# Layer norm 1 of a small vision transformer read from PSUM, with the position rows folded into the patch products, and a new order of work behind it

## What is computed

```python
h = einsum('bnf,of->bno', patches, W) + b + pos_emb           # 768 -> 256
h = h + attention(layernorm(h))      # 16 heads of 16, causal with ALiBi bias, inside each image
h = h + ffn(layernorm(h))
# ffn: r = relu(bitlinear(x, w_fc) + gate * (x @ v.T @ fast_b.T @ u.T)); bitlinear(r * r, w_proj)
# bitlinear(x, w): w rounded to -1, 0, 1 times a scale of its row; layernorm without gain, eps 1e-5
```

## Time and profile before

| | us |
|---|---|
| median of 3 runs | 68.41 (68.33 to 68.67) |
| the profiled execution, its own time | 68.16 |
| its span in the trace | 66.4 |
| TensorE busy | 58.6 |
| VectorE busy | 45.3 |
| ScalarE busy | 38.6 |
| GpSimd busy | 25.9 |

### The profile page before, as it was taken

The page is one execution under the profiler, slowest core; times in us unless marked ns, Lnnn a source line. Parts: engine busy times, 40 slices in busy tenths (PEclk is TensorE's granted clock), DMA queues, the critical chain, the costliest instruction groups (busy, mean ns, idle before and its releaser), DMA issues.

```text
span 66.4 us, 2165 instructions
## 1 busy us (share of the span) xinstructions
PE 58.6 (88%) x894; PEld 53.1 (80%) x894; DVE 45.3 (68%) x97; ACT 38.6 (58%) x78; POOL 25.9 (39%) x43
## 2 busy tenths in 40 slices
PE   5989999999989999999947958999988999999900
PEld 5968588889968999698936846999978999999800
DVE  0000039467999896999799993725999589989660
ACT  5300012824294969974899699830988599783000
POOL 6500007597779569999957100000000000000840
PEclk9999999999999999999999999999999999999996
DMA  0899999999810000000000000000000000000044
GB/s 0 238 352 340 320 392 400 344 387 400 320 42 0 10 0 0 0 10 0 10 0 0 10 5 5 0 10 0 0 0 0 0 0 0 0 0 0 10 161 156
DMA packets 3371, 6.50 MB, mean 98 GB/s; under 512 B 385, under 2 KB 1314, under 8 KB 3362
## 3 DMA queue, kind: packets, MB, share of 16 engines
q1 hardware_dynamic: 3218, 6.24, 26.4%
q10 hardware_dynamic: 144, 0.13, 0.6%
HBM read 5.85 MB, written 0.52 MB: 96 GB/s over the span
## 4 chain that ended last, share of the span: by engine, by line
PE 60%; DVE 18%; ACT 10%; DMA 5%; issue 3%
PE psum L307 12%; PE psum L467 12%; PE psum L493 11%; PE psum L373 5%; PE psum L347 5%; DMA head_sb<-head 5%; PE psum L313 3%; PE psum L402 3%; DVE z L787 3%; PE psum L476 2%; PE psum L327 2%; DVE prob_n L850 2%; DVE bn L779 2%; DVE prob_t L857 2%; ACT zt_hi L610 2%
## 5 line engine op out<-in xcount | busy, mean ns | idle before, releaser
L1051 POOL TENSOR_TENSOR tail_sb<-tail_sb,h 128x256 f32<-128x256 f32 x3 | 2.1, 734 | 25.0 <-DVE tail_sb L886 25.0
L493 PE MATMUL psum<-mlp_t,sq_lo 128*128 128x256 f32 x32 | 7.7, 281 | 0.0
L493 PE MATMUL psum<-mlp_t,sq_hi 128*128 128x256 f32 x32 | 7.7, 280 | 0.0
L601 ACT ACTIVATE std<-mv,eps_sb 128x1 f32<-128x1 f32 x8 | 2.4, 294 | 8.8 <-DVE mv L781 8.8
L777 DVE TENSOR_TENSOR h<-psum,posb 128x256 f32<-128x256 f32 x4 | 1.6, 412 | 8.5 <-PE psum L307 8.5
L467 PE MATMUL psum<-zt_hi,fc_t 128*128 128x256 f32 x32 | 6.9, 287 | 0.5 <-ACT zt_hi L610 0.5
L726 ACT ACTIVATE head_sb<-psum,fc_scale 128x256 f32<-128x256 f32 x16 | 6.7, 471 | 0.7 <-DVE kqv_sb L897 0.7
L467 PE MATMUL psum<-zt_lo,fc_t 128*128 128x256 f32 x32 | 6.7, 279 | 0.0
L493 PEld LDWEIGHTS psum<-mlp_t,sq_lo 128*128 128x128 f32 x32 | 6.0, 189 | 0.0
L493 PEld LDWEIGHTS psum<-mlp_t,sq_hi 128*128 128x128 f32 x32 | 6.0, 189 | 0.0
L307 PE MATMUL psum<-head_sb 128*128 128x256 f32 x24 | 5.7, 389 | 0.3 <-DMA head_sb<-head 0.3
...
## 6 DMA issues: line engine op xcount, KB each, us to landing
...
```

The costliest lines, as they stand in the source:

```text
L493: mm = pe.matmul(mlp_ps[f * BH + b], part[:, n % RING, a, b * P:(b + 1) * P], mlp_t[:, 2 * j + a, :], start=j == 0 and a == 0 and i == 0 a ...
L601: nc.scalar.activation(std[:, which, b:b + 1], mv[:, which, b, 1:2], ACT.Sqrt, bias=eps_sb[:, 0:1]).then_inc(std_ready, 1)
```

## The change

- The position rows are stored twice, 17 rows from partition 0 and again from partition 32 (49 rows in all). ACT rounds them to fp32r, DVE replaces the lower copy's vectors by the low part, and one fp32r product for each block adds both to `tok_ps[b]` as the last of its sum. The fp32 product L509 and `posb` are gone.
- `stats1` and `normalise1` read `tok_ps[b]` in PSUM. ACT copies each block to h (`hidden_copy`) behind its z; the products that reuse these banks wait for the copies, and so does `residual`.
- DVE spreads no keys: ACT takes heads 0 and 3 of half 0, POOL heads 1 to 3 of half 1. DVE copies k of half 1, which was ACT's. ACT makes `ident_bf` and `select_r`, which were POOL's.
- DVE's order: z of block 3 ahead of the key copy, both `fc_sums` ahead of the low part of the second turned z, `rows_sum(0)` behind the two divisions.
- Layer norm 2: both std ahead of `mlp_signs(0)`, the copy of the turned z ahead of `duo_rows(1)`, `mlp_signs(1)` later. On TensorE `turn_mlp(1)` stands behind `project(1)`, `hidden_low(0, 0)` ahead of it, `mlp_out(0, 0)` ahead of `hidden_main(1, 0)`.
- POOL squares step 0 (`SQ_POOL`), DVE the other seven; `residual(1)` moves behind POOL's weight work.

```diff
+POS_LOW = 32
+POS_ROWS = POS_LOW + S + 1
...
-        posb = sb("posb", [P, E])
+        pos_sb = sb("pos_sb", [POS_ROWS, P + E])
+        pos_r = sb("pos_r", [POS_ROWS, P + E], F32R)
...
-        z2t_ps = [bank[2], bank[3]]
-        low_ps = [bank[2][:, 0:HT], bank[4][:, 0:HT]]
-        FCB = [bank[i] for i in (0, 1, 2, 0, 5, 1, 2, 0)]
+        z2t_ps = [bank[1], bank[3]]
+        low_ps = [bank[1][:, 0:HT], bank[4][:, 0:HT]]
+        FCB = [bank[i] for i in (0, 2, 1, 0, 5, 1, 2, 0)]
...
+        SQ_DVE, SQ_POOL = (1, 2, 3, 4, 5, 6, 7), (0,)
...
-                return pe.matmul(tok_ps[b], lhs, head_sb[:, k, HT:HT + E], start=k == 0, stop=k == KF - 1)
+                return pe.matmul(tok_ps[b], lhs, head_sb[:, k, HT:HT + E], start=k == 0, stop=False)
+
+            def embed_pos(b, stop=False):
+                return pe.matmul(tok_ps[b], pos_r[:, 0:P], pos_r[:, P:P + E], start=False, stop=stop)
...
-            pe.wait_ge(pos_in, 16)
-            pe.matmul(pos_ps, pos_sb[:, 0:P], pos_sb[:, P:P + E], start=True, stop=True).then_inc(pos_done, 1)
-            for b in range(BH):
-                for k in range(LAST, KF):
-                    pe.wait_ge(head_in[k], 16)
-                    mm = embed(k, b)
-                mm.then_inc(tok_done, 1)
+            for k in range(LAST, KF):
+                pe.wait_ge(head_in[k], 16)
+                for b in range(BH):
+                    embed(k, b)
+                    if k == KF - 1:
+                        pe.wait_ge(pos_step, 2)
+                        embed_pos(b, stop=True).then_inc(tok_done, 1)
             pe.wait_ge(tail_in[0], 16)
             for k in range(KF):
-                mm = embed(k, 2)
-            mm.then_inc(tok_done, 1)
+                embed(k, 2)
+            embed_pos(2, stop=True).then_inc(tok_done, 1)
...
+            embed_pos(3, stop=True).then_inc(tok_done, 1)
             key(0)
             query(0)
             turn(1, z, zt_ps[1], z1_ready, zt_turned)
+            pe.wait_ge(h1_ready, 3)
             value(0)
             score_bias(0)
             scores(0)
             pe.wait_ge(k_copied, 1)
+            pe.wait_ge(h1_ready, BLOCKS)
             key(1)
...
+            turn(0, z, z2t_ps[0], z2_ready, z2t_turned)
             pe.wait_ge(mlpt_ready, 1)
-            turn(0, z, z2t_ps[0], z2_ready, z2t_turned)
             spread_scale()
-            pe.wait_ge(duo_ready, 6)
-            turn_mlp(1)
             hidden_main(0, 0, (z2t_hi,))
             hidden_main(0, 1, (z2t_hi,))
             low_rank(0)
             hidden_main(0, 0, (z2t_lo,))
             hidden_main(0, 1, (z2t_lo,))
+            hidden_low(0, 0)
             project(1)
-            hidden_low(0, 0)
+            turn_mlp(1)
             hidden_low(0, 1)
             hidden(0, 2)
             pe.wait_ge(relu_ready, 2)
-            hidden_main(0, 3)
+            hidden(0, 3)
             pe.wait_ge(row_copied, 1)
             turn(1, z, z2t_ps[1], z2_ready, z2t_turned)
-            hidden_low(0, 3)
             pe.wait_ge(mlpt_ready, 2)
+            mlp_out(0, 0)
             hidden_main(1, 0, (z2t_hi,))
-            mlp_out(0, 0)
             low_rank(1)
             hidden_main(1, 0, (z2t_lo,))
             mlp_out(0, 1)
             hidden_low(1, 0)
+            pe.wait_ge(relu_ready, 6)
             hidden_main(1, 1)
             hidden_low(1, 1)
-            pe.wait_ge(relu_ready, 6)
             hidden(1, 2)
...
+            def hidden_copy(b):
+                act.wait_ge(z1_ready, b + 1)
+                nc.scalar.activation(h1[:, b, :], tok_ps[b], ACT.Copy).then_inc(h1_ready, 1)
+
+            act.wait_ge(pos_in, 16)
+            nc.scalar.activation(pos_r[:, :], pos_sb[:, :], ACT.Copy).then_inc(pos_step, 1)
             norm_std(0, 0, var1, std1)
             norm_std(1, 0, var1, std1)
+            act.wait_ge(const_in, 16)
+            nc.scalar.activation(ident_bf[:, :], ident, ACT.Copy).then_inc(ident_half, 1)
             weight_high(K, k_in, k_w_hi)
             weight_high(Q, q_in, q_w_hi)
             copy_out(zt_hi[0][:, :, :], zt_ps[0][:, :], zt_turned, 1, zt_hi_ready)
             norm_std(2, 0, var1, std1)
             weight_high(V, v_in, v_w_hi)
+            nc.scalar.activation(select_r[:, :, :], select.rearrange("p (o s) -> p o s", o=1).broadcast_to(
+                [P, HPG, S]), ACT.Copy).then_inc(select_done, 1)
+            hidden_copy(0)
+            hidden_copy(1)
             norm_std(3, 0, var1, std1)
-            key_spread(0, (0,))
+            hidden_copy(2)
+            hidden_copy(3)
+            key_spread(0, (0, 3))
             query_copy(0)
             copy_out(zt_hi[1][:, :, :], zt_ps[1][:, :], zt_turned, 2, zt_hi_ready)
             value_copy(0)
             nc.scalar.activation(table_junk[:, :], eps_sb[:, :], ACT.Exp)
             mlp_sums(0)
-            key_copy(1)
             exponentials(0)
...
+            norm_std(1, 1, var2, std2)
             mlp_signs(0)
-            norm_std(1, 1, var2, std2)
+            copy_out(z2t_hi[0][:, :, :], z2t_ps[0][:, :], z2t_turned, 1, z2t_hi_ready)
             duo_rows(1)
-            copy_out(z2t_hi[0][:, :, :], z2t_ps[0][:, :], z2t_turned, 1, z2t_hi_ready)
-            mlp_signs(1)
-            copy_out(scale_row[:, :], row_ps, row_done, 1, row_copied)
...
-            norm_std(2, 1, var2, std2)
+            copy_out(scale_row[:, :], row_ps, row_done, 1, row_copied)
             relus(0)
-            norm_std(3, 1, var2, std2)
             squares(0)
             relus(1)
-            copy_out(z2t_hi[1][:, :, :], z2t_ps[1][:, :], z2t_turned, 2, z2t_hi_ready)
+            norm_std(2, 1, var2, std2)
+            norm_std(3, 1, var2, std2)
+            mlp_signs(1)
             squares(1)
             relus(2)
-            low_high(1)
+            copy_out(z2t_hi[1][:, :, :], z2t_ps[1][:, :], z2t_turned, 2, z2t_hi_ready)
             relus(3)
             squares(2)
+            low_high(1)
             squares(3)
...
+            def stats(b, which, hidden_state, bn_sem, var_sem):
+                dve.bn_stats(bn6[:, which, b, :], hidden_state).then_inc(bn_sem, 1)
...
+                dve.tensor_scalar(z[:, b, :], hidden_state, mv[:, which, b, 0:1], rstd[:, which, b:b + 1],
...
+                dve.wait_ge(tok_done, b + 1)
+                stats(b, 0, tok_ps[b], bn1, var1)
 
             def normalise1(b):
-                normalise(b, 0, h1, std1, rstd1, z1_ready)
+                normalise(b, 0, tok_ps[b], std1, rstd1, z1_ready)
...
-            dve.wait_ge(posb_ready, 1)
+            low_rows = slice(POS_LOW, POS_ROWS)
+            low_part(pos_r[low_rows, P:P + E], pos_sb[low_rows, P:P + E], pos_r[low_rows, P:P + E], 1, pos_step, pos_step)
             stats1(0)
             stats1(1)
             normalise1(0)
             normalise1(1)
+            stats1(2)
             zt_low(0)
-            stats1(2)
             normalise1(2)
             stats1(3)
+            normalise1(3)
             key_copy(0)
-            normalise1(3)
-            key_spread(0, (3,))
             fc_sums(0)
-            zt_low(1)
             fc_sums(1)
             scales(fc_sum, fc_scale, 2, E, fc_summed, fc_scaled)
             low_rank_factors()
+            zt_low(1)
             softmax_shift(0)
-            key_spread(1, (3,))
+            key_copy(1)
             softmax_sum(0)
             softmax_divide(0, 0)
             softmax_divide(0, 1)
-            softmax_turn(0)
+            softmax_turn(0, 0)
+            softmax_turn(0, 1)
             softmax_shift(1)
             scales(mlp_sum, mlp_scale, KE, HID, mlp_summed, mlp_scaled)
             softmax_sum(1)
             softmax_divide(1, 0)
+            softmax_divide(1, 1)
             rows_sum(0)
-            softmax_divide(1, 1)
-            softmax_turn(1)
+            softmax_turn(1, 0)
+            softmax_turn(1, 1)
...
-            square(0)
-            square_low(0)
-            z2t_low(1)
             square(1)
             square_low(1)
+            z2t_low(1)
...
-                pool.wait_ge(z1_ready, BH * (f + 1))
+                pool.wait_ge(h1_ready, BH * (f + 1))
...
+            def square(n):
+                r, i, old = n % PART_RING, SQ_POOL.index(n), n - PART_RING
+                pool.wait_ge(relu_ready, 2 * n + 2)
...
+                                   ALU.mult).then_inc(sq_pool, 1)
+                pool.wait_ge(sq_pool, i + 1)
...
+                                   ALU.subtract).then_inc(sq_lo_pool, 1)
 
...
             key_spread(0, (1, 2))
-            pool.wait_ge(k_spread_dve, 1)
             residual(0)
-            residual(1)
             hidden_factors()
-            key_spread(1, (1, 2))
+            key_spread(1, (1, 2, 3))
             rounds(fc_sb, fc_scale, fc_whole, range(KH), fc_scaled, fc_rounded)
             rounds(mlp_sb, mlp_scale, mlp_whole, range(KE), mlp_scaled, mlp_rounded)
             value_factors()
+            residual(1)
+            for n in SQ_POOL:
+                square(n)
```

(6 more changed lines are left out.)

82 lines of the change are left out of this document (36 added, 46 removed).

## The result

The changed kernel takes 70.24 and 70.26 us, the kernel before 68.33 to 68.67 us on the same chip: a ratio of 1.026. With a further execution of 71.26 us, in which TensorE's granted clock was 0.971 of full speed on average, it is 1.031 [1.017, 1.045]. That is slower; whether by more than 2% the interval leaves open. The forecast was 68.8 us (67.6 to 69.5), so the time lies 0.7 us above the range. Some executions of every kernel here take some per cent longer, often with a lower granted clock, and times and ratios leave them out where nothing else is said.

The account below looks back on a forecast made before the run. TensorE, busy 88% of the span, was taken as the bound. Shift 0.0 at the turned z's copy plus 0.4 to 0.45 late gave 68.6 profiled from 68.16, or 68.8 us with 0.25 for the median; range 67.6 to 69.5.

Parts of the forecast that it names:

- Start: First stage on TensorE: dropping the fp32 position product gains nothing, four cheap products come in, key products start 0.6 late.
- Four products of 0.118 come in: First stage: one position product of 0.118 us behind each block, three ahead of the first half's turn, +0.35.
- What the fp32 product gave back: Start: removing the fp32 position product (0.69 as a record) gains nothing, as the next load still waited 0.33 for its transfer.
- the larger transfer: Start: the position transfer grows from 25.5 to 73.5 KB ahead of the last two head pieces, 0.12 to 0.15 us.
- Layer norm 1: DVE saves the 0.42 sum per block; TensorE's 0.44 wait for z goes, net +0.15 at scores of half 0.
- No difference: Layer norm 1: statistics and z from PSUM take no longer, bounded by 0 and +0.1 per instruction.
- Scores of half 1: POOL's third key spreading, slowed by meeting DVE's softmax divisions, ends at 28.0; these scores start +0.6 late.
- rival without a meeting: POOL's spreadings and DVE's divisions do not meet, spreadings end at 27.7: 68.3 us, chance 0.22.
- Middle: From scores to the copy of the turned z in norm 2: the shift falls from +0.6 to 0.0.
- Late stage: After the turned z's copy: eight turns +0.45, waits 1.0 against 0.9 before, less 0.1: +0.4 to +0.45.
- GpSimd's square: Late stage: POOL's work for step 0 ends at 48.3, TensorE asks at 49.9; covered by 1.6, costs nothing.
- Rivals: No meeting (0.22), ACT keeps up late, 67.6 (0.21), POOL held in full, 69.3 (0.15), ACT losing its 0.4 cover early.

Follow-up runs that it names:

- e1: The kernel before with a position transfer of 49 rows instead of 17, the rows beyond 17 not read: ratio 1.000 [0.994, 1.005] to the kernel before.
- d1: The changed kernel with the old start (one fp32 position product, added by DVE): 69.17, 69.18, 69.93 and 69.99 us.
- d2: The changed kernel with the old start, ACT's copy of the second turned z before block 2's relus, and DVE spreading head 3 of half 1: 68.23 and 68.55 us.
- b4: The changed kernel with the old start (one fp32 position product, added by DVE), one execution in which the clock fell: 71.71 us.
- b1: The changed kernel with position products zero-padded to 128 rows and the old order behind norm 2, GpSimd keeping step 0's square: 71.89 to 73.44 us.

## Why the prediction was wrong

- **Start: the step that failed.** "Four products of 0.118 come in" took the price of a 128x256 product from a piece of 40 such products in a row. Each cost 0.12 + 0.39 = 0.51, so four cost 2.0 where 0.47 was in the sum: 1.5 of the 1.64 us by which the profiled time (70.24 for 68.6 forecast) was missed. The trace of before had nearer rows. One is the score bias, 64 rows: in the chain two products stand with 0.31 where two of 128 rows take 0.23, and as records they have 379 ns where 128-row ones have 280:

```profile
L357 PE MATMUL psum<-bias_t,select_r x4: 379/379/380, 20.9 to 26.9; 64*128 64x256 f32 x4
```

The other is the old position product itself, with 17 rows. It took 0.62 in the chain, where six products of 128 rows took 2.59, 0.43 each, and the prediction read the 0.33 behind it in the earlier trace rows as a wait for the head transfer, since the view names one. With the same start, the profiles of e1, d1, d2 and b4 have the same 0.33 in front of this product's load and behind it, where no transfer is named. First e1:

```profile
8.00 0.29 PEld L509 LDWEIGHTS psum<-pos_sb 17*128 17x128 f32 x2 [0.33 <-issue]
8.63 1.38 PEld L307 LDWEIGHTS psum<-head_sb 128*128 128x128 f32 x7 [0.33 <-issue]
```

The 20 records of the embedding behind it took 4.54 before (4.51 in e1), and 4.32 behind padded products. So the earlier trace rows most likely held the surcharge that the sum left out.

- **What the fp32 product gave back.** Nothing, said the prediction, and its ground, that 0.33, was misread. The outcome stays open: without any position product the first turn is at 12.58, with the fp32 product it was at 12.53, but the head transfers move this point by more between executions. The 0.12 for the larger transfer is too small for e1 to show.
- **Layer norm 1.** Right in the main: the wait of TensorE for z of block 3 is gone. "No difference" from PSUM was wrong by little: z takes 0.54 from PSUM and 0.41 from SBUF for 256 columns, statistics 0.43 from either; the bound was +0.1 for each, so z is 0.03 over it. It was covered. The Trainium skill ("VectorE: DVE Perf Modes", Why PSUM operands drop a tier) has a PSUM operand cap fp32 at single rate. An estimate from that page: a drop from double to single rate would double the time. The measured step is 1.3 times, and the measurement decides.
- **Scores of half 1.** Right in the mechanism: the three spreadings were to take 2.43 (25.57 to 28.0) by the meeting of GpSimd and VectorE, and took 2.48. Between the scores of the two halves the shift was to grow by 0.45 and grew by 0.67 (2.09 - 1.42). The third spreading took 1.12 beside divisions of up to 1.17, the first two 0.69. The rival without a meeting (chance 0.22) fell.
- **Middle.** Forecast -0.6 between scores and copy, measured -0.74. Right, by the path that was named: the first division of half 1 was to take 0.95 instead of 1.37 and took 0.97.
- **Late stage.** The waits came where they were put, and the eight turns stood in full load with 0.45. But the sum was +0.45 and the stage costs 0.76. By the idle time of the weight loads TensorE waited 0.27 for the low rank part (0.3 forecast; its low part ends 0.11 ahead of the load), 0.56 for the second turned z (0.45) and 0.19 for its low part (0.24), in sum 1.02 for a forecast of 1.0 (timeline, PEld):

```profile
45.83 0.30 PEld L479 LDWEIGHTS psum<-low_t,u_t 128*128 128x128 f32 x2 [0.27 <-issue]
...
52.90 0.53 PEld L470 LDWEIGHTS psum<-zt_hi,fc_t 128*128 128x128 f32 x4 [0.56 <-issue]
53.63 0.19 PEld L456 LDWEIGHTS psum<-zt_hi,v_fold 128*128 128x128 f32 x1 [0.19 <-issue]
```

In the kernel before the same measure gives 0.72, in the one wait ahead of 50.04, where the sum had 0.9 for before. So about 0.2 of the missing 0.3 is this term, the waits that were already there. The other 0.1 is argued from small pieces, as the two products behind the bfloat16 turns (0.31 where two take 0.23). No run isolates it.

- **GpSimd's square** was covered, as said. It ends at 49.7, and the last two normalizations follow at 50.1; b1 shows the price if they meet.
- **Rivals.** All four were about waits and engines; none was about the price of an added instruction in its place. With the products padded, the time (68.62) is the profiled forecast of 68.6 almost to the digit, but by luck: in that profile the scores of half 0 start at 20.95, 0.4 sooner than forecast, the middle is 0.15 cheaper, and the second spreading (0.2) and the late stage (0.4) are dearer.
